# A mixer's decay-spreading products: from one 128-row form to two 32-row forms side by side

## What is computed

```python
dt = softplus(dt + dt_bias); A = -exp(A_log); dA = exp(dt * A)
h  = h * dA[:, :, None, None] + dBx      # step by step along the tokens
y  = einsum('bhpn,bn->bhp', h, C_t)
```

## Time and profile before

| what | value |
|---|---|
| runs of the kernel before, median of 3 | 2783.55 us (2783.29 to 2788.19) |
| the profiled execution | 2785.11 us |
| its span, first to last instruction | 2783.1 us |
| mean granted TensorE clock | 0.992 of full |
| instructions | 42307 |

### The profile page before, as it was taken

How to read it: one execution, slowest core, us unless ns; L and a number is a source line. 1 busy time by engine, 2 the same in 40 slices (tenths; PEclk the granted TensorE clock), 3 DMA queues, 4 the chain that set the end, 5 groups by cost and what they waited for, 6 DMA issues and landing times.

```text
span 2783.1 us, 42307 instructions
## 1 busy us (share of the span) xinstructions
PE 2681.1 (96%) x15264; PEld 2078.4 (75%) x15264; DVE 1531.4 (55%) x2567; ACT 1029.8 (37%) x2385; POOL 638.6 (23%) x564
## 2 busy tenths in 40 slices
PE   6999999999999999999999989999999998999998
PEld 4777777777777888888888867777777776777775
DVE  6887887797795321332232377777777773111222
ACT  6244244344344222122212255555555553222221
POOL 0633643553551101010001001332223321000000
PEclk8999999999999999999999999999999999999999
DMA  4011011001114101110112130111011123211111
GB/s 135 16 46 46 0 45 45 25 20 45 46 46 137 61 0 60 60 60 0 60 60 87 31 107 9 61 60 40 28 60 53 67 82 122 76 45 45 45 45 46
DMA packets 85417, 147.82 MB, mean 53 GB/s; under 512 B 3968, under 2 KB 17920, under 8 KB 85344
## 3 DMA queue, kind: packets, MB, share of 16 engines
q1 hardware_dynamic: 85344, 146.84, 15.2%
HBM read 113.27 MB, written 33.55 MB: 53 GB/s over the span
## 4 chain that ended last, share of the span: by engine, by line
PE 86%; DVE 8%; issue 2%; ACT 2%; DMA 1%; POOL 0%; DVEq 0%; SPq 0%; POOLq 0%; ACTq 0%
PE ps L75 22%; PE ps L77 22%; PE ps L76 22%; PE ps L1662 4%; PE ps L1972 4%; PE ps L736 3%; PE ps L1674 2%; DVE mx_cv L543 1%; PE ps L1653 1%; DVE mx_m L551 1%; PE ps L712 1%; DVE at_pT L1525 1%; PE ps L724 1%; PE ps L1682 1%; DVE at_r_hl L1532 1%
## 5 line engine op out<-in xcount | busy, mean ns | idle before, releaser
L1369 ACT ACTIVATE at_pr<-ps,at_nm 128x256 f32<-128x256 f32 x512 | 236.3, 474 | 191.6 <-DVE at_nm L1519 191.6
L1066 DVE TENSOR_TENSOR gm_m_lo<-gm_m,gm_m_hi 128x512 fp32r<-128x512 f32 (+1 forms) x88 | 61.0, 693 | 416.6 <-ACT gm_m_hi L983 416.6
L75 PE MATMUL ps<-sh_u_hi,gm_gu_hi 128*128 128x512 f32 (+1 forms) x704 | 275.4, 391 | 1.6 <-DVE gm_gu_lo L213 1.6
L77 PE MATMUL ps<-sh_u_hi,gm_gu_lo 128*128 128x512 f32 (+1 forms) x704 | 275.3, 391 | 0.0
L76 PE MATMUL ps<-sh_u_lo,gm_gu_hi 128*128 128x512 f32 (+1 forms) x704 | 275.1, 391 | 0.0
L1525 DVE COPY at_pT<-ps 128x512 f32<-128x512 f32 x256 | 176.3, 689 | 127.2 <-PE ps L1662 123.9
L977 ACT ACTIVATE gm_sg<-ps 128x512 f32<-128x512 f32 (+1 forms) x88 | 52.7, 598 | 520.9 <-PE ps L77 520.9
L75 PE MATMUL ps<-sh_u_hi,qm_w_hi 128*128 128x512 f32 x512 | 202.7, 396 | 6.1 <-ACT qm_h L1910 6.1
L76 PE MATMUL ps<-sh_u_lo,qm_w_hi 128*128 128x512 f32 x512 | 200.4, 391 | 0.0
L77 PE MATMUL ps<-sh_u_hi,qm_w_lo 128*128 128x512 f32 x512 | 200.4, 391 | 0.0
L491 POOL TENSOR_TENSOR mx_m<-mx_m,mx_g 128x512 f32<-128x512 f32 x128 | 184.8, 1444 | 44.7 <-DVE mx_m L553 44.4
(11 more groups left out here) (243 smaller groups left out, 6311.4 us busy)
## 6 DMA issues: line engine op xcount, KB each, us to landing
sh_xf<-x_scratch SPq DMA_DIRECT2D x16, 1024.0 KB, 7.5
sh_xf<-in_x SPq DMA_DIRECT2D x8, 1024.0 KB, 7.4
mx_xr<-in_x SPq DMA_DIRECT2D x8, 1024.0 KB, 6.2
h_scratch<-mx_xr SPq DMA_DIRECT2D x8, 1024.0 KB, 5.1
sh_xf<-h_scratch SPq DMA_DIRECT2D x8, 1024.0 KB, 8.2
gm_xr<-in_x SPq DMA_DIRECT2D x8, 1024.0 KB, 7.3
gm_r<-h_scratch SPq DMA_DIRECT2D x8, 1024.0 KB, 6.0
x_scratch<-gm_r SPq DMA_DIRECT2D x8, 1024.0 KB, 5.1
```

The source lines that it names most:

```text
L75: nc.tensor.matmul(out, l_hi, r_hi, start=first, stop=False)
L77: return nc.tensor.matmul(out, l_lo, r_hi, start=False, stop=last)
L1369: A(pr[h][:, t, :], SC[h][:, SEQ * t:SEQ * t + SEQ], ACT.Exp, bias=nm[:, 4 * n + h, t:t + 1], accum_out=sums[:, 2 * b + t, 4 * g + h:4 * g ...
```

## The change

The turned tile of decays holds its high and low halves twice, in rows 0 to 31 and again in 32 to 63. An even head's spreading product reads rows 0 to 31, an odd head's rows 32 to 63; neither reads the padding rows. With that: `da_hl` is 64 columns per token tile and the two VectorE operations that fill it write twice as much; the four transpositions have 64 columns of weights; the copy to `daT` and the two memsets of its first columns cover 64 rows; the two memsets that cleared `sel` and `daT` at the start are gone, and the counts of that semaphore with them; and the wait for `dal` stands inside `conv_in(i, 3)`, ahead of its last three products, no longer behind it.

```diff
-    smalls, dve_0 = su.stage(smalls=4, dves=10)
+    smalls, dve_0 = su.stage(smalls=4, dves=8)
...
-    da_hl = sb("da_hl", [P, TT, 2 * NH], F32R)
+
+    da_hl = sb("da_hl", [P, TT, 2, 2 * NH], F32R)
...
-    sel_f = sb("sel_f", [2 * NH, NH])
+    sel_f = sb("sel_f", [4 * NH, NH])
...
-            V.memset(sel[:, :].bitcast(F32), 0.0).then_inc(su.dve, 1)
-            V.memset(daT[:, :].bitcast(F32), 0.0).then_inc(su.dve, 1)
...
-            dve.wait_ge(su.dve, dve_0 + 6)
-            V.tensor_copy(sel[0:2 * NH, :], sel_f[:, :]).then_inc(su.dve, 1)
+            V.tensor_copy(sel[0:4 * NH, :], sel_f[:, :]).then_inc(su.dve, 1)
...
-            V.tensor_copy(da_hl[:, :, 0:NH], d["da"]).then_inc(s["dah"], 1)
+            twice = d["da"].unsqueeze(2).to_broadcast([P, TT, 2, NH])
+            V.tensor_copy(da_hl[:, :, :, 0:NH], twice).then_inc(s["dah"], 1)
             dve.wait_ge(s["dah"], i + 1)
-            V.tensor_tensor(da_hl[:, :, NH:2 * NH], d["da"], da_hl[:, :, 0:NH].bitcast(F32),
+            V.tensor_tensor(da_hl[:, :, :, NH:2 * NH], twice, da_hl[:, :, :, 0:NH].bitcast(F32),
                             ALU.subtract).then_inc(s["dal"], 1)
...
-            V.tensor_copy(daT[0:2 * NH, :], Y[0:2 * NH, :]).then_inc(s["dac"], 1)
+            V.tensor_copy(daT[0:4 * NH, :], Y[0:4 * NH, :]).then_inc(s["dac"], 1)
...
-                V.memset(daT[0:2 * NH, SEQ * b:SEQ * b + 1].bitcast(F32), 0.0).then_inc(s["dac"], 1)
+                V.memset(daT[0:4 * NH, SEQ * b:SEQ * b + 1].bitcast(F32), 0.0).then_inc(s["dac"], 1)
...
-            T.matmul(BC[h % 2][:, :], sel[:, h:h + 1].to_broadcast([P, P]), daT[:, :], start=True, stop=True).then_inc(s["bc"], 1)
+            rows = slice(2 * NH * (h % 2), 2 * NH * (h % 2) + 2 * NH)
+            T.matmul(BC[h % 2][:, :], sel[rows, h:h + 1].to_broadcast([2 * NH, P]), daT[rows, :], start=True,
+                     stop=True).then_inc(s["bc"], 1)
...
-            for n in range(1, 4):
+            for n in range(1, 3):
                 conv_in(i, n)
             at(pe, s["sse"], i)
-            pe.wait_ge(s["dal"], i + 1)
-            for t in range(TT):
-                last = T.transpose(Y[0:2 * NH, P * t:P * t + P], da_hl[:, t, :].bitcast(F32), ident[:, :])
+            conv_in(i, 3, (s["dal"], i + 1))
+            for t in range(TT):
+                last = T.transpose(Y[0:4 * NH, P * t:P * t + P], da_hl[:, t, :, :].rearrange("p c h -> p (c h)").bitcast(F32),
+                                   ident[:, :])
...
-    sel = np.concatenate([np.eye(NH, dtype=np.float32)] * 2)
+    sel = np.concatenate([np.eye(NH, dtype=np.float32)] * 4)
```

More of the change, by code:

```diff
@@ L382, in first @@
             act.wait_ge(su.small, smalls)
-            act.wait_ge(su.dve, dve_0 + 7)
+            act.wait_ge(su.dve, dve_0 + 5)
             A(a_neg[:, :, :], a_log, ACT.Exp).then_inc(su.act, 1)
@@ L594, in main @@
             if step_0(i):
-                dve.wait_ge(su.dve, dve_0 + 10)
+                dve.wait_ge(su.dve, dve_0 + 8)
             V.tensor_tensor(d["dta"], d["dt"], a_neg[:, :, :], ALU.mult).then_inc(s["dta"], 1)
@@ L718, in spread @@
                 if step_0(i):
-                    pe.wait_ge(su.dve, dve_0 + 8)
+                    pe.wait_ge(su.dve, dve_0 + 6)
                 pe.wait_ge(s["dac"], 3 * i + 3)
@@ L757, in main @@
             if step_0(i):
-                pe.wait_ge(su.dve, dve_0 + 9)
+                pe.wait_ge(su.dve, dve_0 + 7)
             for u in (u_hi, u_lo):
```

## The result

The changed kernel takes 2804.35 us (median of 6 runs, 2801.57 to 2806.11) against 2785.01 for the kernel before beside it: ratio 1.0069, interval 1.0056 to 1.0081, 19 us slower. The profiled execution spans 2801.4 us, 18.3 more than before. The sign was forecast, the size was not: 13.2 us, with the range ending at 2802.

What follows compares the result with a forecast made beforehand. TensorE was taken to bound the kernel, except where VectorE paces. Loop pairs 6.2, scan of head 0 0.7 and moved wait 6.3 gave +13.2 us: 2798.3 for the profiled execution, 2796.8 for the median, range 2790 to 2802.

Steps and rivals of the forecast that it cites:

- What bounds the kernel: TensorE, busy 96% of the span, sets the time, except where VectorE paces a stretch of the mixer's steps.
- A pair in the loop: Five pairs a step, heads (6,7) to (14,15): form changes outweigh overlap, +0.155 us each, +6.2 us over eight steps.
- The moved wait: In `conv_in(3)`, TensorE waits for late `dal` ahead of the last three products: +0.90 us a step, +6.3 us in seven.
- Heads 0 and 1: First pair, before VectorE's paced stretch: scan of head 0 starts 0.10 us later, +0.7 us in seven steps.
- Heads (2,3) and (4,5): Pairs in the stretch VectorE paces: getting in and out of the 32-row form falls into idle time, cost 0.
- the first: Rival: 32-row pairs change form without pause, 40 pairs save 0.23 us each, -9.0, `dal` wait stays +6.3; 2780.9 us; chance 0.10.
- the fourth: Rival: neither pauses at the pairs nor late `dal`, -9.0 us, 2774.5 us, faster; chance 0.03.
- The second: Rival: pairs cost as forecast but `dal` isn't late in `conv_in(3)`, +6.9 us, 2790.5 us; chance 0.04.
- The third: Rival: pauses are there and the pair doesn't overlap, because of the second product's own wait, +22.6 us, 2806.1 us; chance 0.07.

Runs made afterwards that it cites:

- experiment 2: Changed kernel with its doubled decays and moved wait, but every spreading product in the 128-row form with zero rows (padded): 2790.74 us, ratio 1.0015 to the kernel before.
- experiment 3: Changed kernel with the first three pairs of each step (heads 0 to 5) in the padded 128-row form: 2796.23 us, ratio 1.0039 to the kernel before.
- experiment 5: Changed kernel with both heads of each pair on rows 0 to 31, so no overlap, and the decays' wait one chunk later: 2809.1 us, ratio 1.0086.
- experiment 1: Changed kernel with the decays' four transpositions and the wait for `dal` one chunk later, the wait in conv_in(4): 2794.5 us, ratio 1.0029 to the kernel before.
- experiment 4: Changed kernel with only the first three pairs 32-row, the others padded to 128 rows, and the decays' wait one chunk later: 2789.65 us, ratio 1.0020.
- experiment 8: Changed kernel with only the pair of heads 0 and 1 32-row, others padded to 128 rows, decays' wait one chunk later: 2786.7 us, ratio 1.0000.
- experiment 9: Changed kernel with only the pair of heads 2 and 3 32-row, others padded to 128 rows, decays' wait one chunk later: 2785.9 us, ratio 0.9995.
- experiment 10: Changed kernel with only the pair of heads 4 and 5 32-row, others padded to 128 rows, decays' wait one chunk later: 2792.28 us, ratio 1.0019.
- experiment 7: Changed kernel with heads 0 to 7 padded to 128 rows, the other four pairs directly behind `chunk_y`, decays' wait one chunk later: 2782.22 us, ratio 0.9992.
- experiment 6: Changed kernel, all pairs 32-row, decays' wait one chunk later, loop pairs of j = 2 to 5 directly behind `chunk_y`: 2796.2 us, ratio 1.0037.

## Why the prediction was right and wrong

- **What bounds the kernel**: right. TensorE's time in the loop counted in full, and the stretch that VectorE paces hid what stood in it, as far as VectorE's own chain goes.
- **A pair in the loop**: right, +0.155 forecast, +0.152 by experiments 2 and 3, +0.16 in the timeline. Overlap (0.22 by experiment 5, 0.235 forecast) and pauses are both there, and getting in and out costs the 0.39 of the forecast (experiment 5). By the Trainium skill ("TensorEngine Tiling (Array Packing)", section "Tiling Modes") a change of mode drains the array. The trace agrees: the loads pause for 0.17 and 0.24 at the two edges.
- **The moved wait**: right in kind, +0.90 forecast, +0.8 by experiment 2, 0.87 by experiment 1. The release took 0.05 (155.87 to 155.92), not the 0.15 that I took from the transpositions. My own numbers there give 154.6 - 153.66 = 0.94 and not 0.92. And the list of waits doesn't confirm today's wait of 0.02: its seven entries at L775 are put down to issue and are 0.27 each.
- **Heads 0 and 1**: +0.10 forecast for the scan, +0.15 measured (experiments 4 and 8), inside the 0.06 to 0.21 that I gave. The scan of the changed kernel starts 0.14 behind the end of the product's record (175.23 + 0.49 = 175.72):

```profile
175.86 1.22 DVE L549 TENSOR_TENSOR_SCAN mx_m<-ps,mx_cols 128x512 f32<-128x512 f32 x1 [0.15 <-PE ps L724]
```

- **Heads (2,3) and (4,5): this step failed.** That "getting in and out falls into idle time: 0" is true of the time at the pairs (experiment 9, and the undisturbed steps of 10, both 101.4) and false of what follows. In the kernel before, TensorE is granted full clock behind this stretch. With the pair of heads 4 and 5 in the new form, the clock falls to the lower level in some of the steps (four of eight in the changed kernel, two to five in the six others that have this pair outside the padded form), and about eight products of `z_in(i, 2)` take nearly twice as long: 1.6 us each time. I costed idle time as free and never asked whether TensorE would keep its full clock behind it.
- **The rivals**: the first and the fourth (no pause) are out, since the loads pause at both edges. The second (`dal` not late) is out by the seven waits. The third, no overlap, gives 2806.1, nearer to the measured 2804.35 than my forecast, but by a wrong way: in the loop the two products do run at once, and without overlap the time is 2809.1 even with the decays never late (experiment 5). None of the four has the clock in it.

In sum over the profiled executions: seven steps at 1.78 and 0.8 in the last make 13.3, against 13.2 forecast. That these are so close is partly luck, as the wait came out 0.03 a step cheaper and the scan 0.05 dearer. The halved clock adds 1.4, 1.6, 1.6 and, in the last step, some 1.2, together 5.8. The first pair stands 0.7 earlier (66.3 against 67.1); it stands anywhere from 66.0 to 68.0 in the thirteen profiles, so I draw nothing from it. That makes 18.4, against the 18.3 measured.

**Open:** what about this pair tips the clock. It is shown that for the later steps the pair of heads 4 and 5 is enough by itself (experiment 10), that neither of the two pairs ahead of it is enough alone (8 and 9), and that the five behind it aren't either (3). By the rows at experiment 10, neither more idle time nor overlap is the reason. Whether it is the fewer rows or the pause before the loads is not shown. Nor is why one step is hit and the next is not, or why the first step can be hit with padded products alone (experiment 2). The fall doesn't come at one fixed product: in the rows above, the first slow one is the fourth of `z_in(i, 2)` (394.30) in the changed kernel and the first (287.52) in experiment 10.

## What to carry to other kernels

Packing two thin products side by side saves one slot (0.22 us for 512 columns), and a lone pair between full-array products pays for two changes of form (0.39 us). So put the pair next to something that changes form anyway (experiment 7), or pack where more than two stand together, as in the attention's rows of 24; by these two numbers three would just gain (0.44 against 0.39), which is an estimate, as no run here has three. A wait moved ahead by three products costs what the waited-for work is late, in each step where it is late; look first at when that work ends. And before calling a change in an engine's idle time free, look whether TensorE keeps its clock behind it: here it cost 1.6 us each time, behind a pair that cost nothing itself.

## What the runs showed of the hardware

- A change between the 128-row and the 32-row form idles the weight loads, for 0.17 us on the way in behind transpositions and 0.24 on the way out, and exposes the next load (0.34 from L75 to L76 in place of 0.23). The transpositions with 64 columns of weights (L776) don't cause it: in the changed kernel L75 starts 0.35 behind the first of them (156.73 to 157.08), as it did behind those with 32 columns (154.37 to 154.72).
- Two 32-row products of 512 columns on different rows start together and take 0.50 with their load. On the same rows the pair takes 0.72 (experiment 5).
- The granted clock fell from 2.4 to 1.2 GHz, for some 3 us, behind a stretch in which TensorE's longest idle time was 0.75 us; with the pair there in the 128-row form it stayed up over the same idle time (0.74). In the changed kernel this was in four of eight steps of the same work, and in experiments 4 and 6 in every other step, from the third and from the second on.
